# Rope and transposes of a tile emitted inside the q-k-v loop of an attention stage

## The reference

```python
x = x + 0.5 * ffn(layernorm(x))
x = x + attn(layernorm(x))
x = x + 0.5 * ffn(layernorm(x))

def attn(x):                                 # 16 heads of 64, rope over all 64
    q, k, v = split_heads(x @ qkv_w.T + qkv_b)
    q, k = rope(q), rope(k)                  # e*cos - o*sin, e*sin + o*cos on even/odd pairs
    p = softmax(q @ k.T * 64 ** -0.5)
    return merge_heads(p @ v) @ proj_w.T + proj_b
```

## Time and profile before

| what | us |
|---|---|
| median of the two runs | 12146.99 |
| the two runs | 11655.70, 12638.28 |
| the profiled execution's own time | 11655.7 |
| its span on the slowest core | 11654.2 |
| spans of the eight cores | 11631.0 to 11654.2 |
| PE busy with matmuls | 9274.3 (80%) |
| VectorE busy | 2569.1 (22%) |
| ScalarE busy | 2729.5 (23%) |

### The profile page before, as it was taken

One profiled execution on the slowest core, in us unless ns is written; L12 is line 12 of the kernel. 1 busy time (PEld: TensorE's weight loads), 2 busy tenths in 40 slices (PEclk: granted clock), 3 DMA queues, 4 the chain that ended last, 5 costly groups with the idle time before them and its releaser, 6 DMA issues.

```text
span 11654.2 us, 117172 instructions; the slowest of 8 cores (11631.0 to 11654.2 us)
## 1 busy us (share of the span) xinstructions
PE 9274.3 (80%) x43072; PEld 4171.3 (36%) x43072; DVE 2569.1 (22%) x5933; ACT 2729.5 (23%) x3492; POOL 530.3 (5%) x1004
## 2 busy tenths in 40 slices
PE   5999998399999935655746765589999957999996
PEld 2444443144444412222222222234444423444442
DVE  3111111311111133444344344321111122111111
ACT  1222221122222204332413442212222211222221
POOL 0000000000000000000000000000000000000000
PEclk9999999699999966666766666799999978999998
DMA  2132112211311130000110000402113130211131
GB/s 62 30 56 32 29 32 51 90 29 29 58 29 29 29 103 6 1 6 6 53 40 6 6 1 6 114 19 44 29 29 58 30 83 31 52 36 29 30 58 56
DMA packets 183132, 442.92 MB, mean 38 GB/s; under 512 B 21432, under 2 KB 46136, under 8 KB 182592
## 3 DMA queue, kind: packets, MB, share of 16 engines
q0 software_dynamic: 140976, 284.34, 14.8%
q1 hardware_dynamic: 41616, 151.08, 3.8%
HBM read 669.28 MB, written 50.33 MB: 62 GB/s over the span
## 4 chain that ended last, share of the span: by engine, by line
PE 70%; ACT 11%; DVE 7%; DMA 6%; issue 4%; POOL 1%; SPq 0%; DVEq 0%; ACTq 0%; POOLq 0%
PE p2psog L428 15%; PE p2psh L382 14%; PE p0psog L428 14%; PE p0psh L382 14%; ACT ptw L731 7%; PE psav L696 5%; PE psstq L583 3%; DMA xt<-x2scratch 2%; DMA xt<-x 2%; ACT L406 1%; DMA xt<-x1scratch 1%; DMA p0w1bf<-w 1%; ACT p2hsb L406 1%; PE psstq L587 1%; DVE xt L486 1%
## 5 line engine op out<-in xcount | busy, mean ns | idle before, releaser
L428 PE MATMUL p0psog<-p0w2bf,p0hsb 128*128 128x512 bf16 x8192 | 1778.4, 379 | 69.9 <-ACT p0hsb L406 63.3
L428 PE MATMUL p2psog<-p2w2bf,p2hsb 128*128 128x512 bf16 x8192 | 1778.3, 379 | 69.3 <-ACT p2hsb L406 65.5
L382 PE MATMUL p0psh<-xnfm,p0w1bf 128*128 128x512 bf16 x8192 | 1797.3, 380 | 41.5 <-ACT p0hsb L406 32.7
L382 PE MATMUL p2psh<-xnfm,p2w1bf 128*128 128x512 bf16 x8192 | 1797.5, 380 | 33.7 <-ACT p2hsb L406 32.2
L428 PEld LDWEIGHTS p0psog<-p0w2bf,p0hsb 128*128 128x128 bf16 x8192 | 797.0, 98 | 1051.3 <-issue 99.7
L428 PEld LDWEIGHTS p2psog<-p2w2bf,p2hsb 128*128 128x128 bf16 x8192 | 797.0, 98 | 1050.6 <-issue 99.0
L382 PEld LDWEIGHTS p0psh<-xnfm,p0w1bf 128*128 128x128 bf16 x8192 | 795.4, 98 | 1032.2 <-issue 91.2
L382 PEld LDWEIGHTS p2psh<-xnfm,p2w1bf 128*128 128x128 bf16 x8192 | 795.8, 98 | 1022.9 <-issue 79.9
L447 DVE SCALAR_TENSOR_TENSOR p0accum<-p0psog,p0wsel,p0accum 128x512 f32<-128x512 f32 x512 | 384.5, 751 | 3170.3 <-PE p0psog L428 3170.3
L447 DVE SCALAR_TENSOR_TENSOR p2accum<-p2psog,p2wsel,p2accum 128x512 f32<-128x512 f32 x512 | 384.6, 751 | 3160.3 <-PE p2psog L428 3160.3
L406 ACT ACT_TABLE_LOAD x128 | 164.2, 1283 | 3817.9 <-PE p0psh L382 1913.9
(11 more groups left out here) (107 smaller groups left out, 3308.3 us busy)
## 6 DMA issues: line engine op xcount, KB each, us to landing
p0w1bf<-w POOLq DMA_DIRECT2D x128, 512.0 KB, 17.2
p0w2bf<-w POOLq DMA_DIRECT2D x256, 256.0 KB, 14.8
p2w1bf<-w POOLq DMA_DIRECT2D x128, 512.0 KB, 14.6
p2w2bf<-w POOLq DMA_DIRECT2D x256, 256.0 KB, 12.3
xt<-x SPq DMA_DIRECT2D x64, 512.0 KB, 4.6
xt<-x1scratch SPq DMA_DIRECT2D x64, 512.0 KB, 4.6
xt<-x2scratch SPq DMA_DIRECT2D x64, 512.0 KB, 4.3
x1scratch<-xt SPq DMA_DIRECT2D x32, 512.0 KB, 2.9
```

The lines of the kernel that those rows point to most:

```text
L382: ins = t.matmul(psum_h[pb][:, 0:512], w1bf[dc][:, 128 * hc:128 * (hc + 1)], xn_fm[dc][:, 512 * tj:512 * (tj + 1)], start=(dc == 0), stop= ...
L428: ins = t.matmul(psum_og[ob][:, 0:512], hsb[hc][:, 128 * t128:128 * (t128 + 1)], w2bf[hc][:, 512 * oh:512 * (oh + 1)], start=(hc == 0), st ...
```

## The change

The bodies of the three loops over the tiles stay as they are but for one added wait. They are put into two functions and emitted in another order: the q-k-v matmuls and casts of tile i, then rope, transposes and copies of tile i-1, and for the last tile these three at the end.

```diff
-            for i in range(nts):
+            def emit_tile_qkv(i, hg=hg):
                 def pe_q(t, i=i, hg=hg):
...
                 env.dve(dve_q)
 
-            for i in range(nts):
+            def emit_tile_ropetr(i, hg=hg):
                 for off in (0, 256):
                     def dve_r(v, i=i, off=off):
+                        v.wait_ge(env.sDVE.h, g[("vaug_rdy", i)])
                         tset = ropet[(2 * i + off // 256) % 3]
...
                     env.dve(dve_r)
 
-            for i in range(nts):
                 def pe_t(t, i=i):
...
                     g[("qkfm", i)] = env.sDVE.n
                 env.dve(dve_t)
+
+            for i in range(nts):
+                emit_tile_qkv(i)
+                if i >= 1:
+                    emit_tile_ropetr(i - 1)
+            emit_tile_ropetr(nts - 1)
```

## The result

| | us |
|---|---|
| before, median of 12 runs | 12403.48 (11655.70 to 12876.42) |
| changed, median of 13 runs | 12512.03 (12192.28 to 12973.66) |
| ratio, changed to before | 1.0704, 95% interval 1.0654 to 1.0753 |
| predicted | 11929, range 11830 to 11990 |

The change makes the kernel slower, the way that was forecast, but the measured time lies above the range. The ratio can't be understood without one thing: it is that of three runs of the changed kernel whose cores all show a mean granted clock of 0.81 to 0.83 (12442.09, 12489.02 and 12512.03 us) to three of the kernel before at 11,656 to 11,665 us (0.876 in the one profiled), while the ratio of the medians of all runs is 12512.03 / 12403.48 = 1.009. So the study has two questions: what the change does in the stage that it touches, and what the rest of the 7% is.

The account below looks back on a forecast made before the run. TensorE is busiest overall, but the eight q-k-v blocks (1024.2 us) chain TensorE and VectorE. Per block 9.5 + 4.35 + 143.8 + 4.5 = 162.1 us against 128.0; +273 us on 11655.7 gives 11,929, range 11,830 to 11,990.

Parts of the forecast that it names:

- The loop through both engines: Q-k-v blocks: rope waits for next tile's casts, transposes for rope, next matmuls for transposes; only the copies get hidden.
- The rival of overlap: Q-k-v blocks: a later tile's matmuls run while VectorE ropes; 4.6 us a tile, 11,296 us in all; chance 0.02.
- The gap loses the clock every time: Q-k-v blocks: about 3.8 us of PE idle costs TensorE its high clock in each of the fourteen repeated gaps.
- rival 2: Q-k-v blocks: PE's idle time is short enough to keep the clock; block 129.3 us, 11,666 us in all; chance 0.05.
- One turn: One tile's pass through the PE and VectorE loop in the q-k-v blocks: 10.27 us, between 9.41 and 10.77.
- The late rise: Clock returns to 2.4 GHz before the end of 0.70 of the tile bursts, saving 0.5 us a burst.
- The block and the sum: First q-k-v to first score matmul: 162.1 us against 128.0, +34.1 a block, +273 us for eight.
- The low clock throughout: Q-k-v blocks: every turn stays at 1.2 GHz, 10.77 us; block 169.1 us, 11,984 us in all; chance 0.18.
- forgiven gaps: Q-k-v blocks: half of the idle gaps keep the clock; 11,798 us in all; chance 0.10.
- no clock lost: Q-k-v blocks: no gap costs the clock; turn 7.92 us, +1.3 us a block, 11,666 us in all; chance 0.05.
- rival 1: Q-k-v blocks: all turns at the low clock, 10.77 us each; +41.1 us a block, 11,984 us; chance 0.18.
- the rule named beside it: Trainium skill's HAM oscillation section: matmul bursts alternating with waits lose the clock in every wait and start cold; gives 11,984 us.

## Why the prediction was right and wrong

- **The loop through both engines.** Right: rope waits behind the next tile's casts, the transposes behind rope, the next matmuls behind the transposes; moving rope one place took 82 us out of a block. The rival of overlap fell as argued, by the order on PE.
- **The gap loses the clock every time.** Right, and it is more than the whole cost: 36.4 us a block by the filled gap, of which the new order gives 3.7 back. That the rows of the output projection give the point from which a gap is forgiven (rival 2) was wrong: six filling matmuls leave mostly 1.9 to 2.3 us idle, less than the 2.46 that had kept the clock there, and still 58 to 63% of the turns lost it.
- **One turn.** 10.27 us predicted, 10.21 measured in the mean, by two errors that nearly cancel. The gap was put at 4.35 us and is about 4.1: from the cast of v to the first rope product 0.36 instead of 0.48, and from the first transpose to the next matmul 0.37 instead of 0.52, since the row for the latter ended on a score matmul. The late rise was to save 0.5 us a burst and saves 0.3 in the mean (10.51 in a turn without it, 10.21 over all). That 0.70 of the bursts would see it came out: 984 of 1,344 (0.73) over twelve cores of undisturbed dies.
- **The block and the sum.** 162.1 predicted, 160.7 measured; +273 us predicted, +261 measured in the blocks. That 11,925.28, in the run that had both dies undisturbed, lies 4 us from 11,929 is partly luck: the kernel before took 11,665 beside it, 9 us more than the base of the prediction. The granted clock of the blocks was 0.56 to 0.68, not near 0.55, since much of the high clock fell into the gaps. The added wait was costed at nothing and cost nothing.
- **The low clock throughout, forgiven gaps, no clock lost.** Not borne out: on the profiled core 0 the clock rose in 63 of 112 bursts, so neither did every burst stay low, as rival 1 and the rule named beside it had it, and no gap of the full length kept it.
- **What failed.** The step "the profiled execution's own time is 11655.7 us, ... my number stands against 11655.7", and with it the range. It took the feed-forward clock of that one execution for granted in all others. The other run shown, 12638.28, said otherwise, and that spread was named and then not used. The feed-forward phases are some 8,400 of 11,650 us (4,190 for the first alone), and in the stretch above the same work goes 8,018 / 6,695 = 1.20 times slower at a clock of 0.81; the losses seen reach 13,311.67 - 11,925 = 1,387 us, five times the whole effect of the change. A range for the time of a run would have had to reach from about 11,900 to 13,300; the range given holds for the difference alone.
- **Elsewhere nothing.** On undisturbed dies it holds: from one block to the next (the score stage) 235 to 237 us before and after. The ratio of 1.07 is not a cost of the change; the part that is, is 1.021 to 1.025.

## What to carry to other kernels

When two stages are interleaved on in-order engines, write down the list of each engine for one turn and ask what stands in front of the next independent piece: here one place on VectorE made the difference between 160.7 and 79.0 us a block. Work that is split into bursts with waits of some microseconds between them can cost more by TensorE's clock than by the waits; filling the gap with useless matmuls is a quick test of that. And where the runs of the kernel before lie 8% apart, find out which stage and which die the spread is in before a number is put on a change elsewhere.

## What was not expected of the hardware

- One die can take up to some 1,390 us longer for the program than it does at other times, on equal work, with granted clocks down to 0.81 in dense feed-forward stretches; which die it is changes from run to run. Within the die the loss comes on pairs of neighbouring cores, mostly at different times, and yet all four end together.
- Adding 210 matmuls of 128x512 to a block made it 36 us shorter.
- Three such matmuls a gap cost and gain nothing (160.8 against 160.7 us); six gain 16 us even on a die with the lower clock; 14 gain 36.
- An idle time of 1.9 us kept TensorE's clock in one turn and lost it in the next.
